# One core, eight chunks of attention plus experts: the first projection in halves, two tiles normalised on another engine, and other orders

## The reference

```
xn = (x - mean) / sqrt(var + 1e-5)
# attention, per batch of 256 rows; lw = 1/(|i-j|+1e-7) off the diagonal, 0 on it
p   = exp(tanh(((xn @ W + b) @ xn.T) * lw));  p[diagonal] = 0
att = (p / (sum(p) + 1e-7)) @ xn
# experts: 8, the best 2 per row by sigmoid(xn @ gate_w.T) + bias; width 176 each
h   = sum over the chosen e of  relu(score_e * xn @ up_e.T)^2 @ down_e.T
hs  = relu(xn @ shared_up.T)^2 @ shared_down.T
out = x + att + h + hs
```

## Time and profile before

| | |
|---|---|
| median of three runs | 119.6 us |
| the profiled execution's own time | 119.29 us |
| its span (first to last instruction) | 117.5 us |
| PE busy | 110.8 us (94%) |
| DVE busy | 100.7 us (86%) |
| ACT, POOL busy | 89.7, 71.4 us |
| granted PE clock | 1.00 of full speed throughout |

### The profile page before, as it was taken

The page is one execution under the profiler, slowest core; times in us unless marked ns, Lnnn a source line. Parts: engine busy times, 40 slices in busy tenths (PEclk is TensorE's granted clock), DMA queues, the critical chain, the costliest instruction groups (busy, mean ns, idle before and its releaser), DMA issues.

```text
span 117.5 us, 2790 instructions
## 1 busy us (share of the span) xinstructions
PE 110.8 (94%) x912; PEld 84.1 (72%) x912; DVE 100.7 (86%) x316; ACT 89.7 (76%) x138; POOL 71.4 (61%) x121
## 2 busy tenths in 40 slices
PE   3987899999999999999999999999999999999981
PEld 3935438877869776869578777879588757778770
DVE  6997989995998999989898989899898689987741
ACT  4463789959769897889798797889689878896730
POOL 6549996797974897529971797549870504371000
PEclk9999999999999999999999999999999999999999
DMA  2999214666669919494759949693959566698991
GB/s 85 309 242 327 102 34 89 128 123 123 123 131 125 213 24 207 96 177 85 146 100 200 118 84 184 119 143 78 170 112 208 102 112 133 133 202 50 201 239 62
DMA packets 47821, 16.56 MB, mean 141 GB/s; under 512 B 44992, under 2 KB 45760, under 8 KB 47808
## 3 DMA queue, kind: packets, MB, share of 16 engines
q1 hardware_dynamic: 47232, 15.44, 68.4%
q0 software_dynamic: 288, 0.72, 3.2%
q10 hardware_dynamic: 288, 0.23, 0.7%
HBM read 3.84 MB, written 2.10 MB: 51 GB/s over the span
## 4 chain that ended last, share of the span: by engine, by line
PE 81%; DMA 8%; DVE 4%; ACT 3%; issue 1%; POOL 1%; DVEq 0%; POOLq 0%; ACTq 0%
PE out_ps L981 15%; PE h_ps L934 13%; PE side L910 10%; PE dots L889 10%; DMA hiddenT<-hidden 8%; PE out_ps L969 6%; PE small L879 4%; PE side L923 4%; PE small L861 4%; PE out_ps L963 4%; PE out_ps L1011 4%; PE small L846 2%; PE side L879 2%; PE h_ps L947 2%; DVE gated L676 1%; ACT projT L439 1%
## 5 line engine op out<-in xcount | busy, mean ns | idle before, releaser
L676 DVE SCALAR_TENSOR_TENSOR gated<-h_ps,gates 128x1408 bf16<-128x1408 f32 x28 | 45.4, 1621 | 5.3 <-PE h_ps L934 4.9
L491 ACT ACTIVATE hidden<-gated 128x1408 bf16<-128x1408 bf16 x30 | 40.7, 1377 | 6.0 <-DVE gated L676 4.9
L981 PE MATMUL out_ps<-downT,hiddenT 128*128 128x128 bf16 x341 | 22.8, 219 | 0.6 <-DMA hiddenT<-hidden 0.5
L981 PEld LDWEIGHTS out_ps<-downT,hiddenT 128*128 128x128 bf16 x341 | 20.8, 98 | 2.7 <-DMA hiddenT<-hidden 1.0
L262 POOL TENSOR_SCALAR xn<-x_sb,meanvar,rstd 128x128 f32<-128x128 f32 x28 | 22.0, 795 | 0.8
L934 PE MATMUL h_ps<-upT,xnTb 128*128 128x512 bf16 (+1 forms) x84 | 21.3, 362 | 0.3 <-DVE gated L676 0.3
L295 POOL TENSOR_SCALAR_AFFINE_SELECT probs<-probs 128x256 f32<-128x256 f32 x16 | 6.5, 408 | 16.9 <-ACT probs L448 16.9
L910 PEld LDWEIGHTS side<-xn,probs 128*128 128x128 f32 x120 | 15.2, 191 | 1.8 <-issue 1.0
L889 PE MATMUL dots<-projT,xnT 128*128 128x256 f32 x60 | 15.6, 383 | 0.6 <-ACT projT L439 0.6
L910 PE MATMUL side<-xn,probs 128*128 128x129 f32 x120 | 15.8, 274 | 0.0
L889 PEld LDWEIGHTS dots<-projT,xnT 128*128 128x128 f32 x60 | 10.8, 190 | 4.9 <-ACT projT L439 2.4
(11 more groups left out here) (107 smaller groups left out, 170.2 us busy)
## 6 DMA issues: line engine op xcount, KB each, us to landing
x_sb<-in_x SPq DMA_DIRECT2D x7, 256.0 KB, 9.1
out_y<-final SPq DMA_DIRECT2D x7, 256.0 KB, 2.7
hiddenT<-hidden SPq DMA_TRANSPOSE x31, 3.7
upT<-in_up POOLq DMA_DIRECT2D x1, 352.0 KB, 7.5
downT<-in_down POOLq DMA_DIRECT2D x1, 352.0 KB, 8.4
out_y<-final SPq DMA_DIRECT2D x2, 128.0 KB, 1.7
late_sb<-in_late SPq DMA_DIRECT2D x1, 192.0 KB, 6.4
x_sb<-in_x ACTq DMA_DIRECT2D x1, 128.0 KB, 2.6
```

Source lines behind the costliest of these rows:

```text
L491: a.activation(hidden[:, t, :], gated[:, t, :], ACT.Square).then_inc(squared, 1)
L676: v.scalar_tensor_tensor(out=gated[:, t, :].rearrange("p (e h) -> p e h", e=E), in0=h_ps[:, 0:NH].rearrange("p (e h) -> p e h", e=E), scal ...
L981: last = t_.matmul(out_at(t), hiddenT[:, c % 2, t, j, :], downT[:, j, :], start=(t == 0 and j == 0 and c < LAST), stop=((t >= 2 or c == LA ...
```

## The change

In the new kernel the lines are other ones; the functions keep their names. What it does:

- **First projection.** Chunk 0's projection is made in two halves of 256 columns (`project_first`, copied by `take_first_proj`). The first needs only the half of `xnT` that DVE copies; `dots(0,0)` needs only the first half, `rest(0)` starts its first half before ACT's copy.
- **Second chunk.** Tiles 2 and 3 of chunk 1 are normalised by DVE (`normalize_second`), tiles 0 and 1 by POOL.
- **Bank.** Chunk 0's turned exponentials go to the second output bank, not to `h_ps`; the wait for them moves from `up_tile(0, 0)` to `dots(0, 1)`.
- **Orders.** All four engines' lists change for the first three chunks, in the loop and for the last chunk. There ACT squares tiles 0 and 1 ahead of `relu_shared` and `scale_attention`.

Of the orders the diff shows the loop and the end of DVE, ACT and PE; the start is shown as lists behind it.

```diff
         def exp_bank(c):
-            return small[:, S:2 * S] if c else h_ps[:, 0:S]
+            return small[:, S:2 * S] if c else out_ps[:, CH:CH + S]
...
+            def take_first_proj(half):
+                act.wait_ge(early_loaded, 16)
+                act.wait_ge(proj_made if half else first_proj_made, 1)
+                cols = slice(half * S, (half + 1) * S)
+                a.activation(projT[:, 0, cols], side[:, cols], ACT.Identity, bias=b_sb
+                             ).then_inc(proj_taken if half else first_proj_taken, 1)
...
+            def normalize_second(t):
+                dve.wait_ge(rstd_ready, 1)
+                v.tensor_scalar(xn[:, 1, t, 0:D], x_sb[:, 1, t, :], meanvar[:, 1, t, 0:1],
+                                rstd[:, 1, t:t + 1], ALU.subtract, ALU.mult).then_inc(second_xn_ready, 1)
...
+            def project_first(half):
+                pe.wait_ge(early_loaded, 16)
+                if half:
+                    pe.wait_ge(xT_taken, 1)
+                else:
+                    pe.wait_ge(first_half_taken, 1)
+                cols = slice(half * S, (half + 1) * S)
+                t_.matmul(side[:, cols], W_sb, xnT[:, 0, cols], start=True, stop=True
+                          ).then_inc(proj_made if half else first_proj_made, 1)
...
             for k in range(3, NCH):        # ACT
                 f, c = k, k - 1
+                exp_logits(f)
                 relu_rest(f)
-                exp_logits(f)
...
                 take_proj(f)
+                relu_shared(c)
                 take_pair(f)
-                relu_shared(c)
                 square(c, 2)
                 take_tanh(f, 0)
                 take_exp(f, 0)
-                square(c, 3)
                 if f + 1 < NCH:
                     take_xT(f + 1)
+                square(c, 3)
...
+            square(LAST, 0)
+            square(LAST, 1)
             relu_shared(LAST)
             scale_attention(LAST)
-            square(LAST, 0)
-            square(LAST, 1)
...
                 f, c, o, g = k, k - 1, k - 2, k + 1        # DVE
                 gate(c, 0)
                 attend_sums(c, 0)
+                attend_norm(c, 0)
                 if g < NCH:
                     norm_stats(g)
-                attend_norm(c, 0)
                 gate(c, 1)
                 route_one(f)
                 finish(o, 0)
+                attend_sums(c, 1)
                 route_scores(f)
-                attend_sums(c, 1)
+                attend_norm(c, 1)
                 route_bias(f)
-                attend_norm(c, 1)
                 attend(c)
...
                 gate(c, 3)
+                finish(o, 1)
                 weigh(f, 1)
-                finish(o, 1)
...
                 attend(c, 0)        # PE
+                rest(f)
                 shared_down_rest(o)
-                rest(f)
                 up_tile(c, 1)
...
             up_by_bank(0)
-            shared_main(c)
-            attend(c, 0)
-            up_by_bank(1)
             shared_down_rest(o)
             shared_down_main(o)
+            up_by_bank(1)
+            attend(c, 0)
+            shared_main(c)
             up_by_bank(2)
-            attend(c, 1)
             down_tile(o, 2)
             down_tile(o, 3)
             up_by_bank(3)
             shared_down_rest(c)
             shared_down_main(c)
+            attend(c, 1)
```

More of the change, by code:

```diff
@@ L495, in _ @@
             copy_decay()
+            take_first_proj(0)
+            exp_logits(0)
             relu_rest(0)
-            exp_logits(0)
-            take_proj(0)
+            take_first_proj(1)
             take_pair(0)
+            take_xT(1)
             take_tanh(0, 0)
             take_exp(0, 0)
-            take_xT(1)
-            square(0, 0)
             relu_rest(1)
@@ L507, in _ @@
             take_tanh(0, 1)
+            square(0, 0)
+            take_exp(0, 1)
+            take_tanh(1, 0)
             square(0, 1)
-            take_exp(0, 1)
             relu_shared(0)
-            take_tanh(1, 0)
+            take_xT(2)
             take_pair(1)
+            take_exp(1, 0)
             scale_attention(0)
-            take_exp(1, 0)
             square(0, 2)
-            take_xT(2)
             scale_second()
+            relu_rest(2)
+            exp_logits(2)
             take_tanh(1, 1)
-            exp_logits(2)
-            relu_rest(2)
             take_exp(1, 1)
@@ L526, in _ @@
             take_pair(2)
-            square(1, 2)
             take_tanh(2, 0)
             take_exp(2, 0)
+            square(1, 2)
             relu_shared(1)
-            square(1, 3)
             take_xT(3)
             take_tanh(2, 1)
+            square(1, 3)
             take_exp(2, 1)
@@ L743, in _ @@
             route_scores(0)
+            normalize_second(2)
             route_bias(0)
+            normalize_second(3)
             route_top(0)
@@ L752, in _ @@
             route_one(1)
+            weigh(1, 0)
+            gate(0, 2)
             route_scores(1)
-            gate(0, 2)
             route_bias(1)
-            weigh(1, 0)
             attend_sums(0, 0)
@@ L769, in _ @@
             route_one(2)
+            gate(1, 1)
             route_scores(2)
-            gate(1, 1)
             route_bias(2)
             attend_sums(1, 1)
-            attend_norm(1, 1)
             route_top(2)
-            attend(1)
             gate(1, 2)
             weigh(2, 0)
+            attend_norm(1, 1)
             route_mark(2)
+            attend(1)
             finish(0, 0)
@@ L820, in _ @@
                           turn_at(1)[:, 0:(to - at) * P]).then_inc(turned_taken[1], 1)
+            attend_sums(LAST, 1)
+            attend_norm(LAST, 1)
+            attend(LAST)
             finish(LAST, 0)
-            attend(LAST)
             finish(LAST, 1)
@@ L881, in dots @@
             def dots(c, q):
-                pe.wait_ge(proj_taken, c + 1)
+                if c == 0 and q == 0:
+                    pe.wait_ge(first_proj_taken, 1)
+                else:
+                    pe.wait_ge(proj_taken, c + 1)
+                if c == 0 and q == 1:
+                    pe.wait_ge(expT_taken, 1)
                 if c == 1 and q == 0:
@@ L1015, in _ @@
             transpose_x(0)
+            project_first(0)
             rest(0)
-            project(0)
             transpose_exp(0)
             dots(0, 0)
+            project_first(1)
             up_tile(0, 0)
+            transpose_x(1)
             dots(0, 1)
-            transpose_x(1)
-            shared_main(0)
-            up_tile(0, 1)
             rest(1)
             project(1)
+            up_tile(0, 1)
             transpose_exp(1)
+            shared_main(0)
+            dots(1, 0)
             up_tile(0, 2)
-            dots(1, 0)
             attend(0, 0)
+            dots(1, 1)
             transpose_x(2)
             up_tile(0, 3)
-            dots(1, 1)
             attend(0, 1)
             down_tile(0, 0)
+            rest(2)
             up_tile(1, 0)
@@ L1038, in _ @@
             down_tile(0, 1)
-            rest(2)
             shared_down_rest(0)
-            shared_down_main(0)
             transpose_exp(2)
             up_tile(1, 1)
+            shared_down_main(0)
             project(2)
             attend(1, 1)
-            down_tile(0, 2)
             up_tile(1, 2)
             dots(2, 0)
+            down_tile(0, 2)
+            down_tile(0, 3)
+            up_tile(1, 3)
+            transpose_x(3)
+            dots(2, 1)
             shared_main(1)
-            transpose_x(3)
-            up_tile(1, 3)
-            dots(2, 1)
-            down_tile(0, 3)
             down_tile(1, 0)
```

61 lines of the change are left out of this document (30 added, 31 removed).

## The result

| | before | after | ratio (95%) |
|---|---|---|---|
| median, 20 runs each | 119.56 us | 118.62 us | 0.9924 (0.9905 to 0.9944) |
| median, the changed kernel again (e0_again): 18 runs before, 7 after | 119.2 us | 118.53 us | 0.994 (0.9917 to 0.9964) |

The change makes the kernel 0.9 us faster; 118.7 was predicted. Every ratio here leaves out the executions over 1.5% above the fastest of their kernel, while the medians are of all. The profiled execution of the changed kernel is not a typical one: it took 119.68 us, 1.06 more than the median. Read against the earlier trace rows it would say that nothing was gained.

A forecast was written before the change was run, and what follows sets the result against it. PE was taken to bound the kernel, without a hole in the middle. Start -1.23, loop +0.35 and end 0 summed to -0.9, so 119.6 us became 118.7, with a range from 118.0 to 119.9.

The forecast's parts named there:

- Start, -1.23: First three chunks: up(2,0), chunk 2's first up tile on PE, starts at 35.63 instead of 36.86 us.
- the wait: At the start, PE waiting for the second turning DMA ahead of down(0,1); if slow, it takes back 1.0 us.
- the walk: Step-by-step timing of the new start's lists from profiled durations, with 0.05 us per met wait and 0.1 per unhidden load.
- the turn of chunk 1: PE's turn of chunk 1's normalised tiles at the start: ends at 11.9 us, not before 13.0 previously, -1.1.
- "-0.77": Chunk 0's first dots on PE start at 9.16 instead of 9.93 us, after the projection's first half.
- The cover that may fail: Chunk 0's later squares delay its turning DMAs; median landings stay hidden from PE's down tiles, a slow one costs 1.0 us.
- "3.7 is what most take": Turning DMAs land 3.5 to 5.2 us after issue, 3.7 in the median, so both of chunk 0's were taken as hidden.
- The clock, "it plays no part": Whole kernel: the clock is granted in full everywhere, so it was given no effect.
- Loop, +0.35: PE's weight load for `shared_main` waits for DVE's later attention result: 0.07 us in each of five rounds.
- End, 0: Last chunk: PE's last down tile starts at 114.17 against 114.14 us whatever the DMA does; bounds -0.5 and +0.3.
- The sum: Whole kernel: -1.23 + 0.35 + 0 = -0.9 us, giving 118.7 us on the scale of the runs.
- -0.23: What the start is still worth if the second turning DMA is slow once more and takes back 1.0 us.

The follow-up runs named there:

- f0: Kernel before with only the changed start (loop and last chunk as before), run again on another chip: 118.17 us, ratio 0.9896.
- f1: Kernel before with the changed start and loop orders, but the scores' reciprocal ahead of the row sums and the last chunk as before: 118.14 us, ratio 0.9892.
- h1: Kernel before with only tiles 2 and 3 of chunk 1 normalised by DVE instead of POOL: 119.19 us, ratio 0.999.
- e1: Changed kernel with one line of DVE's loop put back, the scores' reciprocal ahead of the row sums: 118.15 us, ratio 0.9914.
- f3: Changed start alone, but POOL normalises all four tiles of chunk 1 again: 119.38 us, ratio 1.0009.
- g1: Changed start alone, but the first projection is one matmul over 512 columns with one copy: 117.95 us, ratio 0.9863.
- f2: Kernel before with the changed start and last chunk, loop as before: 118.32 us, ratio 0.9893.
- e2: Kernel before with only the changed start, loop and last chunk as before, first run: 117.48 us, ratio 0.986.
- e3: Kernel before with only the last chunk's changed orders, start and loop as before: 119.38 us, ratio 1.0015.
- g3: Changed start alone with 6 warm-up matmuls instead of 10: median 121.29 us; ratio 0.9942 from the four short runs alone.
- g2: Changed start alone, but ACT squares tile 0 of chunk 0 ahead of chunk 1's projection copy and tanh: 118.54 us, ratio 0.9943.

## Why the prediction was right

- **Start, -1.23 with the wait as its price: right in size (-1.42 without the wait, read from DVE's copy), wrong in one reason.** From up(0,2) to up(2,0) I forecast 18.65 us. On the scale of the earlier trace rows the start alone took 35.36 - 0.16 - 16.58 = 18.62, and 18.63 in f0 and f1. In before and in h1 it is 19.90 and 19.92. e1, whose warm-up took what it did before, can be held against the walk step by step: `dots(0,0)` at 9.24 (forecast 9.16), the turn of chunk 1 over at 11.77 (11.9), up(0,1) at 14.49 (14.41), up(0,2) at 16.81 (16.98). The walk was right in the waits too: f3 shows the turn as the gain's condition. What failed is the weight of the projection's halves. "-0.77" at `dots(0,0)`, measured -0.69, is true as a position, but PE has 0.43 of it still to do behind; g1 shows that less than 0.1 us hangs on it.
- **The cover that may fail: right, and both outcomes occur.** I set it at 1.0 us or nothing. In the nine profiles that have the new start with DVE's tiles and ten warm-up matmuls PE waited 0.88 to 0.96 in three (after, e1, f2) and not in six. (1) came 1.0 us later in those three for the same up(0,2). The mean price is then about 0.3 us, and one profile could have shown either. "3.7 is what most take" holds of the turning DMAs as a whole and not of the second: it took 3.8 to 5.3. With 4.2, the commonest of the quick landings, it is there within 0.05 us of when PE comes to it (e2: 19.43 + 4.2 = 23.6, down(0,1) at 23.65), so that the cover held was in part luck.
- **The clock, "it plays no part": wrong.** The granted clock reads 1.00, but the first matmuls run at half speed, and how long they do moves up(0,2) by 0.66 us between e2 and f0. It did so before the change too (16.96 in before, 17.75 in e3), so it scatters the runs and leaves the difference.
- **Loop, +0.35: right.** 64.74 - 64.33 = 0.41 us, at the wait, the engine and the line that I named, 0.08 us a round; undone in e1, with 0.38 us in the medians.
- **End, 0: right within its bounds.** The changed last chunk takes 13.65 to 13.78 us in its five profiles, the old one 13.57 to 14.17 in nine, so perhaps 0.2 less. Alone it brought nothing that 0.3% could show, and f2 is no faster than f0.
- **The sum.** The start alone measured 0.986 and 0.9896 (-1.7 and -1.2 us), the whole change 0.9924 and 0.994 (-0.9 and -0.7). What is between holds the loop's 0.4, as forecast; the rest of it is scatter. My -1.23 was for a start without the wait, which the fixed points put at -1.42, and with the wait they put it at -0.3 to -0.4, where I had -0.23: both a little too small. The two errors cancel in the sum: with the wait in a third of the executions the start is worth about -1.1, and with the loop -0.7 (an estimate from few profiles), near the -0.9 and -0.7 measured. So the mechanism was right, and the nearness of the number is in part luck.
- The Trainium skill's 350 to 400 GB/s for a transposing DMA (Advanced Engine Details and Errata, X-Bar Transpose) stays unmet: while the second turn's data moves, the DMA engines carry 205 GB/s in after (22 to 23 us) and at most 293 in any quarter of a microsecond of the 14 profiles. Nor is it the rate that makes this DMA late, as the last section shows.

The version to keep is the changed start with before's loop order of the scores' reciprocal. The start alone is 0.986 and 0.9896 of before; with the new loop but that one order, 0.9892. All lie below the change as given (0.9924, 0.994), by 0.3 to 0.8%, though not every interval is clear of its.

## What to carry to other kernels

Where one engine has no hole from some point on, mark that point and the one where its last stage starts, and compare kernels by these: a difference of 0.4 us in a loop stood out to 0.02 us while medians scattered by 0.5. An edit that makes work ready sooner pays only with an order that takes it up sooner, so test the two apart and together. And before explaining a small difference between two kernels, take two profiles of one: here 0.7 us of "cause" was most likely luck of the start.

## What the hardware showed

**PE starts at half speed, and the clock's column doesn't say so.** A warm-up matmul's record is 421 ns at first and 274 ns later, its modelled end included; from one record's start to the next it is 0.21 us and 0.11. In g3 everything runs at half speed until 14 us, a factor of 2 as between 1.2 and 2.4 GHz, while the granted clock reads 1.00 in both stretches. Before it, PE had six warm-up matmuls, until 4.84 us, and then stood still for 1.1 us in all up to 10 us. With ten it came to full speed between about 4.5 and 8 us in every profile, not always at the same moment, and that moment shifts the whole kernel by up to 0.7 us. The Trainium skill (TensorE: Matmul & The Clock Gate, Part 1) says that the engine comes from rest at 1.2 GHz and that the moment of the change differs from run to run; the records agree, and the column doesn't show it.

**The second turning DMA lands late, and not always equally so.** The first takes 3.6 us in every profile, most others 3.5 to 3.7, the second 3.8 (g2), 3.9 (g1), 4.2 (e0, e2, f0, f1, f3) or 5.2 to 5.3 (before, after, e1, e3, f2, g3, h1). PE waits only with the last. The rate is not the reason. The DMA's share and GB/s, the last two figures of a row, us by us in after (issue at 20.30, landing at 25.55), then in e0 (20.36 and 24.6):

```profile
22.00:23.00 1.00, 1.00 (x14) 0.53 (x10) 1.00 (x8) 1.00 (x3) 0.34 (x1) 1.00 1.11 205
23.00:24.00 1.00, 0.84 (x8) 0.75 (x8) 0.96 (x7) 0.65 (x2) 0.53 (x3) 1.00 0.32 67
24.00:25.00 1.00, 0.68 (x7) 0.49 (x5) 0.88 (x1) 1.00 (x4) 1.00 (x2) 1.00 0.12 23
...
22.00:23.00 1.00, 1.00 (x14) 0.58 (x11) 1.00 (x7) 1.00 (x3) 0.39 (x1) 1.00 1.52 47
23.00:24.00 1.00, 0.84 (x7) 0.70 (x7) 1.00 (x7) 0.69 (x1) 0.48 (x2) 1.00 0.96 215
```

In the late ones nearly all data has moved 3.3 us after the issue, and the landing comes 2 us behind it (the 23 GB/s at 24 to 25 us are mostly the next turn's). In e0 the data breaks off for about 1 us, ends 3.8 us after the issue, and the landing follows 0.4 us behind. One more thing goes with it in all 14 profiles: a single packet of the queue that the page calls "instruction" (0.02 MB). It moves 0.6 us after the DMA's issue, ahead of its data, in the seven that land in 3.8 to 4.2 us, and 3.0 to 3.2 us after it, at the end of the data, in the seven that land in 5.2 to 5.3. No run moved that packet, so this is a trace to follow and not a cause shown.
